# Expert tiles of a two-layer mixture kernel: two up-projection chunks to a PSUM bank, tiles turned three ahead

## The reference, cut to what matters

```python
# layer 0: gated experts (two hidden chunks of 128)
h = xf @ w1[e] + b1[e]
hidden = silu(h @ wg[e] + bg[e]) * (h @ wv[e] + bv[e])
y = hidden @ w2[e] + b2[e]
...
# layer 1: plain experts (four hidden chunks of 128)
hidden = gelu(x_norm @ w1[e] + b1[e])
y = hidden @ w2[e] + b2[e]
out = out + combine[:, e:e + 1] * y
```

## Time and profile before

| | us |
|---|---|
| median of the runs shown | 2293.36 |
| span of the profiled execution, first to last instruction | 2495.0 |
| stage 0, first turn to last down-projection, in the profile | 1240.7 to 1516.8 |
| stage 1, the same | 2136.1 to 2442.3 |

### The profile page before, as it was taken

The page is one execution under the profiler, slowest core; times in us unless marked ns, Lnnn a source line. Parts: engine busy times, 40 slices in busy tenths (PEclk is TensorE's granted clock), DMA queues, the critical chain, the costliest instruction groups (busy, mean ns, idle before and its releaser), DMA issues. The chain is left out here.

```text
span 2495.0 us, 41046 instructions
## 1 busy us (share of the span) xinstructions
PE 2001.3 (80%) x13306; PEld 1090.0 (44%) x13307; DVE 1432.7 (57%) x3154; ACT 1092.3 (44%) x1682; POOL 753.8 (30%) x883
## 2 busy tenths in 40 slices
PE   5759999898999899986588886986597871699894
PEld 2421223232232223223376664654365541588883
DVE  4779888686878687713155555742444453234444
ACT  4530666564656465763133443431143431334343
POOL 1240003332333334243244552000004445345442
PEclk9865999998999899987699998999889885799996
DMA  3844132323232322011333333222011321232325
GB/s 133 201 169 68 19 51 26 60 27 60 27 60 26 60 32 55 16 40 58 93 83 83 88 89 119 76 93 67 8 36 50 107 60 56 69 80 76 82 68 213
DMA packets 134782, 180.00 MB, mean 72 GB/s; under 512 B 44592, under 2 KB 87856, under 8 KB 132336
## 3 DMA queue, kind: packets, MB, share of 16 engines
q1 hardware_dynamic: 116208, 138.25, 23.3%
q0 software_dynamic: 18432, 39.88, 4.7%
HBM read 99.04 MB, written 69.01 MB: 67 GB/s over the span
## 5 line engine op out<-in xcount | busy, mean ns | idle before, releaser
L775 DVE TENSOR_REDUCE mx<-bank 128x1 f32<-128x512 f32 x1024 | 640.3, 696 | 140.3 <-PE bank L546 90.3
L722 ACT ACTIVATE P<-bank 128x1024 f32<-128x1024 f32 x512 | 498.0, 1021 | 412.9 <-PE bank L648 327.0
L546 PE MATMUL bank<-ks,qs 96*128 96x512 bf16 x1024 | 374.6, 415 | 62.7 <-DVE mx L775 44.3
L1286 POOL DMA_INDIRECT results<-yo,places x284 | 273.9, 964 | 359.6 <-DVE yo L1276 274.8
L648 PE MATMUL bank<-qs,ks 99*128 99x512 bf16 x1024 | 310.9, 387 | 14.3 <-ACT P L722 13.2
L1202 PE MATMUL bank<-xt,up 128*128 128x256 f32 x1136 | 286.6, 397 | 41.9 <-DVE xt L1253 20.8
L628 PE MATMUL bank<-P,vt 128*32 128x512 f32 x2048 | 277.5, 614 | 1.6 <-ACT P L722 1.6
L2285 POOL DMA_INDIRECT dispatched<-planes,places x128 | 123.1, 962 | 479.0 <-DVE stats L2129 356.3
L1202 PEld LDWEIGHTS bank<-xt,up 128*128 128x128 f32 x1136 | 211.6, 196 | 76.8 <-issue 36.0
L546 PEld LDWEIGHTS bank<-ks,qs 96*128 96x128 bf16 x1024 | 100.8, 99 | 305.7 <-DVE mx L775 204.0
L648 PEld LDWEIGHTS bank<-qs,ks 99*128 99x128 bf16 x1024 | 77.4, 98 | 299.1 <-ACT P L722 195.9
(11 more groups left out here) (298 smaller groups left out, 2582.3 us busy)
## 6 DMA issues: line engine op xcount, KB each, us to landing
xr<-dispatched SPq DMA_DIRECT2D x142, 130.0 KB
qk_parts<-parts SPq DMA_DIRECT2D x16, 768.0 KB, 5.1
qs<-qk_parts SPq DMA_DIRECT2D x84, 128.0 KB
ks<-qk_parts SPq DMA_DIRECT2D x84, 128.0 KB
v_turned<-vt SPq DMA_DIRECT2D x8, 1024.0 KB, 5.6
vt<-v_turned SPq DMA_DIRECT2D x8, 1024.0 KB
bands<-results SPq DMA_DIRECT2D x32, 256.0 KB, 3.8
y<-results SPq DMA_DIRECT2D x32, 256.0 KB
```

Source lines behind the costliest of these rows:

```text
L546: pe.matmul(bank[:, slot, :], qs[par][0:KB, h, c * C:(c + 1) * C], ks[par][0:KB, h, half * HALF:(half + 1) * HALF], start=True, stop=True) ...
L722: act.activation(P[:, x % SLOTS, :], bank[:, 2 * pair:2 * pair + 2, :] .rearrange("p a t -> p (a t)"), ACT.Exp).then_inc(probs_ready, 1)
L775: dve.tensor_reduce(mx[:, k // 2, k % 2:k % 2 + 1], bank[:, slot, :], AX.X, ALU.max).then_inc(unit_freed, 1)
L1286: pool.indirect_dma_start(yd_dram, bass.IndirectOffsetOnAxis(places[:, p, q:q + 1], 0), yo[:, p, q, :], None).then_inc(sent[p], 16)
```

## The change

- `xt` and `up` get four buffers (AHEAD) in place of two, `gate` two for each chunk in place of one.
- Two chunks of an up-projection share a bank: chunks 0 and 1 of tile j go to the two halves of bank 2 + 2 (j % 2), chunks 2 and 3 to those of the next bank. Banks 2 to 5 so hold two tiles. PE waits once for each pair, until the pair of tile j - 2 has been read, and signals once for each pair (`g_ready`); `v_ready` is gone.
- Step j on every engine is `turn(j + 3)`, `middle(j + 1)` (activation, and the product in stage 0), `finish(j)`, `up_project(j + 2)`. PE has no `middle`; ACT and DVE have no `up_project`.
- In `turn` of stage 1, DVE writes `xt` before it copies the up block, where before it copied the block first.
- The first two steps are written out ahead of the loop, which still has eight tiles to a turn; the last five steps stand behind it.

```diff
-    up = sb("up", [C, 2, 4 * C], F32)
+    up = sb("up", [C, AHEAD, 4 * C], F32)
...
-    xt = sb("xt", [C, 2, SLOT], F32)
+    xt = sb("xt", [C, AHEAD, SLOT], F32)
...
-    gate = sb("gate", [C, 2, SLOT], F32)
+    gate = sb("gate", [C, 2, 2, SLOT], F32)
...
-            for r in range(RING):
-                at(first, group, r + 1)
-                at(turn, group, r + 2)
-                at(finish, group, r)
...
+        for r in range(2):
+            at(turn, 0, r)
+            at(up_project, 0, r)
+        at(turn, 0, 2)
+        at(middle, 0, 0)
+
+        def step(group, r):
+            for stage, ahead in ((turn, 3), (middle, 1), (finish, 0), (up_project, 2)):
+                if not isinstance(group, int) or RING * group + r + ahead < TILES:
+                    at(stage, group, r + ahead)
...
         @block.tensor
...
-            def first(j, r, p, h, i):
+            def up_project(j, r, i):
+                a = r % AHEAD
                 pe.wait_ge(xt_copied, j + 1)
                 pe.wait_ge(w_copied, j + 1)
                 for f in range(4):
-                    if not (isinstance(j, int) and j == 0):
-                        if second:
-                            pe.wait_ge(h_ready, (j - 1) * 4 + f + 1)
-                        elif f % 2:
-                            pe.wait_ge(h_ready, (j - 1) * 2 + f // 2 + 1)
-                        else:
-                            pe.wait_ge(gated, (j - 1) * 2 + f // 2 + 1)
-                    ins = pe.matmul(bank[:, 2 + f, 0:SLOT], up[:, p, f * C:(f + 1) * C], xt[:, p, :], start=True, stop=True)
-                    ins.then_inc(g_ready if second or f % 2 == 0 else v_ready, 1)
+                    if f % 2 == 0 and not first_use(j, 2):
+                        pe.wait_ge(h_ready, (j - 2) * NH + (f + 2) * NH // 4)
+                    ins = pe.matmul(bank[:, 2 + 2 * (r % 2) + f // 2, f % 2 * SLOT:(f % 2 + 1) * SLOT],
+                                    up[:, a, f * C:(f + 1) * C], xt[:, a, :], start=True, stop=True)
+                    if f % 2:
+                        ins.then_inc(g_ready, 1)
...
         @block.vector
...
+            def turn(j, r, i):
+                a = r % AHEAD
+                dve.wait_ge(turned, j + 1)
                 if second:
                     e = dve.value_load(table[0:1, 0, bass.ds(j, 1)], min_val=0, max_val=E - 1)
-                    if not (isinstance(j, int) and j < 2):
-                        dve.wait_ge(h_ready, (j - 1) * NH)
-                    dve.tensor_copy(up[:, p], wres[:, bass.ds(e, 1), 0:W2].rearrange("c o n -> c (o n)")).then_inc(w_copied, 1)
-                dve.wait_ge(turned, j + 1)
-                if second:
-                    dve.tensor_scalar(xt[:, p, :], bank[:, p, 0:SLOT], w["ln"][:, 0:1], w["ln"][:, 1:2],
+                    dve.tensor_scalar(xt[:, a, :], bank[:, r % 2, 0:SLOT], w["ln"][:, 0:1], w["ln"][:, 1:2],
                                       ALU.mult, ALU.add).then_inc(xt_copied, 1)
+                    if not first_use(j, AHEAD):
+                        dve.wait_ge(g_ready, (j - AHEAD + 1) * 2)
+                    dve.tensor_copy(up[:, a], wres[:, bass.ds(e, 1), 0:W2].rearrange("c o n -> c (o n)")).then_inc(w_copied, 1)
...
-            over_tiles(dve, turn, first, finish)
+            over_tiles(dve, turn, nothing, middle, finish)
```

More of the change, by code:

```diff
@@ L1124, in experts, with over_tiles, at, first_use @@
     LOADS = 16 * 3
-    def over_tiles(eng, turn, first, finish):
-        def at(step, group, r):
+    def over_tiles(eng, turn, up_project, middle, finish):
+        def at(stage, group, r):
             group, r = group + r // RING, r % RING
[L1133 to L1139, removed]
-            for r in range(RING):
-                at(first, group, r + 1)
-                at(turn, group, r + 2)
-                at(finish, group, r)
[L1144 to L1150, removed]
+            stage(RING * group + r, r, group)
+        for r in range(2):
[7 more added lines that the diff above has]
+                    at(stage, group, r + ahead)
+        for r in range(2):
+            step(0, r)
+        groups = (TILES - 3 - 2) // RING
+        with eng.Fori(0, groups) as group:
+            for r in range(2, RING + 2):
+                step(group, r)
+        for r in range(2, TILES - groups * RING):
+            step(groups, r)
     def nothing(*_):
         pass
+    def first_use(j, n):
+        return isinstance(j, int) and j < n
     with nc.Block() as block:
@@ L1222, in turn @@
                 e = act.value_load(table[0:1, 0, bass.ds(j, 1)], min_val=0, max_val=E - 1)
-                if not (isinstance(j, int) and j < 2):
[L1224 to L1228, removed]
-                    act.wait_ge(y_ready, j - 1)
+                if not first_use(j, AHEAD):
+                    act.wait_ge(g_ready, (j - AHEAD + 1) * 2)
@@ L1230, in first, with middle @@
+                act.activation(up[:, r % AHEAD], wres[:, bass.ds(e, 1), 0:W2].rearrange("c o n -> c (o n)"), ACT.Copy).then_inc(w_copied, 1)
+            def middle(j, r, i):
+                p = r % 2
                 for f in range(NH):
-                    act.wait_ge(g_ready, j * NH + f + 1)
+                    column = f % 2 * SLOT if second else 0
+                    at = bank[:, 2 + 2 * p + (f // 2 if second else f), column:column + SLOT]
                     if second:
-                        act.activation(hidden[:, p, f, :], bank[:, 2 + f, 0:SLOT], ACT.Gelu,
-                                       bias=rec[:, r, f:f + 1]).then_inc(h_ready, 1)
-                    else:
-                        if f == 0:
-                            act.wait_ge(h_ready, j * 2)
-                        act.activation(gate[:, f, :], bank[:, 2 + 2 * f, 0:SLOT], ACT.Silu,
-                                       bias=rec[:, r, 2 * f:2 * f + 1]).then_inc(gated, 1)
@@ L1241, in _ @@
-            over_tiles(act, turn, first, nothing)
+                        if f % 2 == 0:
+                            if f == 0 and not first_use(j, 2):
+                                act.wait_ge(y_ready, j - 1)
+                            act.wait_ge(g_ready, j * 2 + f // 2 + 1)
+                        act.activation(hidden[:, p, f, :], at, ACT.Gelu, bias=rec[:, r, f:f + 1]).then_inc(h_ready, 1)
+                    else:
+                        if f == 0 and not first_use(j, 2):
+                            act.wait_ge(h_ready, (j - 1) * 2)
+                        act.wait_ge(g_ready, j * 2 + f + 1)
+                        act.activation(gate[:, p, f, :], at, ACT.Silu, bias=rec[:, r, 2 * f:2 * f + 1]).then_inc(gated, 1)
@@ L1259, in first, with middle @@
+            def middle(j, r, i):
+                p = r % 2
                 if not second:
-                    if not (isinstance(j, int) and j == 0):
+                    if not first_use(j, 2):
                         dve.wait_ge(y_ready, j - 1)
@@ L1272, in finish @@
                                   rec[:, r, 4:].unsqueeze(1).to_broadcast([C, SQ, C]), ALU.add).then_inc(y_copied, 1)
-                dve.wait_ge(sent[p], h * (16 * SQ))
+                if not first_use(j, 2):
+                    dve.wait_ge(sent[p], (i * (RING // 2) + r // 2) * (16 * SQ))
                 dve.tensor_scalar(places[:, p], xr[:, r, :, C + 1], 0.0, None, ALU.add)
```

36 lines of the change are left out of this document (19 added, 17 removed).

## The result

The changed kernel takes 2297.78 us (median; 2293.08 to 2304.13) against 2292.6 us (2286.59 to 2299.22) before: a ratio of 1.0024 with a 95% interval of 1.0015 to 1.0032, or 3.4 to 7.3 us more. So the change made the kernel a little slower.

A forecast was written before the change was run, and what follows sets the result against it. It took stage 0 as bound by the chain of a tile and SP's loads, level at about 3.2 us, and stage 1 by PE at 3.74 us. 2293.4 - 3.5 (loads) + 2.7 (end of stage 0) = 2292.6 us, range 2270 to 2300.

The forecast's parts named there:

- The freezes: Stretches where several engines stand still in the first profile; 143 to 209 us, inferred to be absent from the runs.
- Rival B: Freezes are in the runs too; the earlier turn absorbs 20.8 us of waits in stage 1: 2275.3 us, chance 0.11.
- the term of SP's load: Stage 0: a load taken as 3.15 us against a chain of 3.20, so 3.5 us gained over 70 steps.
- The end of stage 0: After the last rows land, PE has one finish and one up-projection more: 2.7 us lost.
- Stage 1: Second expert stage: PE alone sets 3.74 us a tile, so nothing to gain: 0.
- The fourth load at the start: Start of stage 1: finish(0) waits for one load more, between 0 and 3.06 us; taken as 0.
- the block copy behind xt: DVE's later copy of the up block in stage 1: 0, covered by a whole tile of 3.74 us on PE.
- The chain of a tile: Stage 0: dependence loop from up-projection through second silu, product and xt copy to the next up-projection, 3.20 us.
- the four up blocks: Four buffers for up blocks: same number of copies, each needed two or more tiles later, so 0.
- Rival A: SP is not the bound in the runs; with loads at 2.87 us or less, stage 0 gains 23.1 us: 2270.3, chance 0.24.
- Rival C: The shared bank is exposed and finish(j + 1) waits: up to 34 us slower in stage 0, 2327 us, chance 0.13.
- The cover: 1.7 us of PE work hiding the wait of at most 0.49 us for a bank's second chunk, so cost 0.

The follow-up runs named there:

- e1: The kernel before, profiled a second time with no edit: span 2287.4 us, median 2292.6 us.
- e3: The changed kernel with both bias tensors side by side, so SP issues two DMAs a tile instead of three: 2259.87 us, 0.9852 of before.
- e12: The changed kernel run again without an edit: 2297.48 us, 1.0023 of the kernel before.
- e10: The changed kernel with the turn at the end of a step and, in stage 1, the block copied before DVE's wait: 2293.37 us, 1.0016 of before.
- e13: The kernel of e10 run again: 2291.87 us, 0.9996 of the kernel before.
- e2: The kernel before with both bias tensors side by side, so SP issues two DMAs a tile instead of three: 2282.28 us, 0.9951 of before.
- e6: The kernel of e2 with DVE, in stage 0, copying xt(j + 2) ahead of the products of tile j + 1: 2281.17 us, 0.9949 of before.
- e8: The kernel of e6 with ACT, in stage 0, copying tile j + 2's up block ahead of tile j + 1's silus: 2258.99 us, 0.9853 of before.
- e4: The changed kernel with its shared banks and four buffers, but the old order of steps: 2347.76 us, 1.0236 of before.
- e9: The kernel of e3 with DVE, in stage 1, reading the register and copying the block before its wait: 2256.77 us, 0.9844 of before.

## Why the prediction was right and wrong

**The freezes are not in the runs: right.** It had been an inference; e1 shows it: the same program, profiled without them, has a span of 2287.4 us. The span lies 1.8 us below the time of its run in e1 (2287.4, 2289.16) and in after (2299.6, 2301.37). The Trainium skill's "Runtime: NRT & Kernel Launch" (The ~15µs preamble/postamble breakdown) has the profile's total time about 6.2 us above the execution time. The spans here lie below it, so no run here shows that gap; the 201.6 us belonged to one execution. Rival B is out. That the parts reached the 201.6 us was luck. Against e1, the disturbed profile is 77 us longer ahead of stage 0, 35 in stage 0, 58 between the two stages and 36 in stage 1. The prediction's 60 to 126, 46 and 37 hold the first, second and last of these; for the stretch between the stages they hold nothing, and only the width of the first made up for it. And the forecast that the next span would be about 2475 was wrong: I took freezes to belong to profiling, and no profile after the first had them.

**The step that failed: the term of SP's load.** The earlier trace rows gave 3.26 us in the loop, the chain 3.20, and hence a gain of 0. I then took 3.15, because the rows stood close behind freezes, and booked 70 x 0.05 = 3.5 us of gain. The loads measure 3.29 in both kernels. So the gain was 0: the order that takes 2.84 us a tile with two DMAs (e3) keeps to the 3.29 of the loads with three. The bound that I had worked out was right, and the wish to correct it was the error: without it the sum would have been 2293.4 + 2.7 = 2296, with the right sign.

**The end of stage 0: right.** 2.7 us forecast, 2.5 measured (11.1 to 13.7), 2.8 in e12, and e10 takes it away. From the last turn to the last result e10 is 2.6 us shorter than the changed kernel, the price of the two pieces of PE's work. Against e1 the 2.5 us are a net figure: there the last turn came 4.1 us after its rows were issued (3.3 after the change), and 7.1 us were left behind it.

**Stage 1: wrong, 0 forecast, 1.4 measured** (1.2 in e12). The fourth load at the start cost nothing, as I had chosen. What I called free was the block copy behind xt, "covered by a whole tile of 3.74 us on PE". At the first two tiles there is no such tile, and the register load that moved behind the wait had no term at all. The first down-projection comes 2.5 us later; 0.2 of it is a turn that is only done earlier, and 1.0 comes back at the end by the loosened wait, which had no term either. That makes 1.3.

**The sum with the measured terms**: 0 for the chain, 0.9 for the loads' own stretch (not forecast, and no larger than e13 scatters), 2.5 behind the last load and 1.4 in stage 1 make 4.8 against 5.2 measured.

**The chain of a tile: right in length, incomplete in its parts.** 3.20 forecast, 3.18 in e2. I followed one chain, over the xt copy, and called the four up blocks worth nothing. A second chain, over ACT's block copy, ended at the same moment; e6 shows that to cut the one is not enough, e8 that to cut both is. ACT's order alone was not run; by the rows of e2 the xt copy would still end only 0.03 us earlier.

**Rival A** had its price right (23.1 us) and its condition: the gain comes once a load is cheaper than PE's tile. e3 against e2 shows 22.4 in the runs, and by the stages 21.2 gained in stage 0 and 1.3 lost in stage 1; the rest lies in stages that scatter. That it would not happen by itself is what the 3.29 say.

**Rival C and the shared bank: right, under this order.** The cover held: in the changed kernel PE's down-projections wait for DVE once in stage 0, 0.3 us, and never in stage 1. e4 measures the uncovered price, 0.43 us a tile. The Trainium skill's "Perfetto Trace Analysis" (Optimizing Tensor Performance, Matmuls) asks that independent matmul groups rotate through different banks. No run here tests that rule by itself. The 3.64 us a tile of e4 come from the one signal for two chunks: the second silu starts 0.43 us later, a quarter of the four chunks' 1.7. What it would cost to read one half of a bank while PE writes the other is not shown. e3 shows no loss, at 2.84 us a tile with two chunks to a bank, where the up-projection runs two tiles ahead.

## What to carry to other kernels

When a loads' queue and a dependence chain stand level, shortening the chain shows nothing until the loads get cheaper, and lead that adds work behind a wait for the last load shows as a loss: make the queue cheaper first, here by merging the two bias DMAs of a tile into one (e2, e3). Before cutting a chain, list every operand that the next step waits for; where two producers end together, moving one is not enough (e6, e8). When the wait conditions of an engine are rewritten, list those that became looser too. A term taken from rows should not be shifted by a guess about the rows.

## What the runs showed of the hardware that I had not expected

- The same program was profiled at 2495.0 us once and 2287.4 the next time.
- SP spends about as long on the issue of a 2 KB DMA as on that of a 64 KB one: in after, the 2 KB load of L1167 is followed 0.65 us later by the 64 KB load of L1168, and that one 0.70 us later by the 130 KB rows of L1169 (1302.08, shown above; timeline of SP):

```profile
1300.73 0.50 SPq L1167 DMA_DIRECT2D rec<-biases  x1
...
1301.38 0.50 SPq L1168 DMA_DIRECT2D rec<-XF  x1
```

- At the start of stage 1 the second up-projection of e9 began 2.3 us sooner after the first turn than in the changed kernel (6.2 against 8.5 us), ran at a granted clock of 0.50 where that one had 1.00, and the first down-projection followed only 0.5 us sooner (10.3 against 10.8).
